# The inverse products of levels 1 to 4 as 32 by 32 tiles instead of 64 by 64 quarters, in a gated delta-rule layer

## What is computed

```python
St = St * jnp.exp(gt)[..., None]
err = jnp.einsum('bhk,bhkv->bhv', kt, St)
St = St + bt[..., None, None] * kt[..., None] * (vt - err)[..., None, :]
ot = jnp.einsum('bhk,bhkv->bhv', qt, St)
```

## Time and profile before

| | |
|---|---|
| median of 3 runs | 10145.46 us (10145.2 to 10145.66) |
| span of the profiled execution | 10143.4 us |
| TensorE matmul busy | 9551.0 us (94%) |
| VectorE busy | 7448.5 us (73%) |
| ScalarE busy | 6863.1 us (68%) |
| GpSimd busy | 3592.4 us (35%) |
| mean granted TensorE clock | 0.973 |

### The profile page before, as it was taken

How to read it: one execution, slowest core, us unless ns; L and a number is a source line. 1 busy time by engine, 2 the same in 40 slices (tenths; PEclk the granted TensorE clock), 3 DMA queues, 4 the chain that set the end, 5 groups by cost and what they waited for, 6 DMA issues and landing times. The chain is left out here.

```text
span 10143.4 us, 303836 instructions
## 1 busy us (share of the span) xinstructions
PE 9551.0 (94%) x104164; PEld 6538.4 (64%) x104164; DVE 7448.5 (73%) x13320; ACT 6863.1 (68%) x15797; POOL 3592.4 (35%) x5963
## 2 busy tenths in 40 slices
PE   4899999999999999999999999999999999996888
PEld 2566767677676766666767666676767666773333
DVE  2687878888788878787888878887888787882111
ACT  1677777777777777777777777777777777771111
POOL 0343434444344434443434434343444443440000
PEclk7899999999999999999999999999999999998999
DMA  1211111111111111111111111111111111111000
GB/s 29 50 38 35 37 35 36 36 35 38 35 37 36 36 36 36 36 37 35 37 35 37 36 34 38 35 37 35 36 36 35 36 36 35 38 35 33 8 8 12
DMA packets 513762, 347.45 MB, mean 34 GB/s; under 512 B 63136, under 2 KB 510752, under 8 KB 512816
## 3 DMA queue, kind: packets, MB, share of 16 engines
q1 hardware_dynamic: 511760, 328.31, 12.9%
q0 software_dynamic: 1088, 4.26, 0.1%
HBM read 289.94 MB, written 42.47 MB: 33 GB/s over the span
## 5 line engine op out<-in xcount | busy, mean ns | idle before, releaser
L1174 POOL TENSOR_TENSOR KB<-KB,tot 128x256 f32<-128x256 f32 x1290 | 1050.1, 814 | 4077.3 <-PE bank L601 4077.2
L1242 DVE SCALAR_TENSOR_TENSOR acc<-bank,hp,acc 128x510 f32<-128x510 f32 (+2 forms) x2331 | 1713.9, 744 | 76.5 <-ACT hnew L870 13.1
L554 PE MATMUL bank<-hn,w_qkv 128*128 (+1 forms) x3108 | 1527.7, 614 | 1.5 <-issue 1.5
L1349 DVE TENSOR_TENSOR invT<-invT,bank 64x128 f32<-64x128 f32 x2576 | 740.2, 287 | 541.3 <-PE bank L645 523.9
L1304 DVE COPY_PREDICATED BIG<-masks,bank 128x512 f32<-128x512 int32 x1032 | 1039.9, 1008 | 76.3 <-DVE BIG L1304 65.5
L887 ACT ACTIVATE Zm<-bank 64x128 f32<-64x128 f32 x2576 | 707.1, 274 | 519.2 <-PE bank L628 504.3
L628 PEld LDWEIGHTS bank<-invE,BIG 64*64 64x64 f32 x20624 | 702.6, 134 | 498.3 <-issue 436.1
L1316 DVE TENSOR_TENSOR QKF<-QKF,tot 128x512 f32<-128x512 f32 x1289 | 913.3, 709 | 16.3 <-PE bank L601 1.0
L645 PEld LDWEIGHTS bank<-invT,Zm 64*64 64x64 f32 x20608 | 707.7, 135 | 335.6 <-issue 287.0
L601 PE MATMUL bank<-QKF,KB 128*64 128x64 f32 x20640 | 886.9, 228 | 0.6 <-DVE QKF L1322 0.4
L653 PEld LDWEIGHTS bank<-ident,invT 128*128 128x128 f32 x5152 | 589.6, 141 | 431.6 <-DVE BIG L1304 271.7
(11 more groups left out here) (205 smaller groups left out, 20308.8 us busy)
## 6 DMA issues: line engine op xcount, KB each, us to landing
bb<-beta_rows SPq DMA_DIRECT2D x520, 128.0 KB, 4.1
states<-StC SPq DMA_DIRECT2D x288, 128.0 KB, 1.9
w_qkv<-in_L_attn_wk_dram SPq DMA_DIRECT2D x260, 128.0 KB, 2.3
w_qkv<-in_L_attn_wq_dram SPq DMA_DIRECT2D x260, 128.0 KB, 2.3
w_qkv<-in_L_attn_wv_dram SPq DMA_DIRECT2D x260, 128.0 KB, 2.2
StA<-states SPq DMA_DIRECT2D x259, 128.0 KB, 2.1
w_o<-in_L_attn_wo_dram SPq DMA_DIRECT2D x257, 128.0 KB, 2.1
w_fb<-in_L_attn_f_b_dram SPq DMA_DIRECT2D x260, 64.0 KB, 3.9
```

Source lines behind the costliest of these rows:

```text
L554: mm = eng.matmul(rows(BK["proj_" + "qkv"[n_]]), w_qkv[:, n_, k, :], hn_v[:, k, :, cols], start=(k == 0), stop=(k == KD - 1))
L1174: eng.tensor_tensor(e_, e_, t_.to_broadcast([P, C, P // (2 * m), m]), ALU.mult).then_inc(ev[f"kb_mul{s}"], 1)
L1242: eng.scalar_tensor_tensor(dst, rows(bk)[:, :, 0:BLK - sh], hp[par][:, w_:w_ + 1], dst, ALU.mult, ALU.add).then_inc(ev[("tap_" if t_ < 2 e ...
L1349: x_ = eng.tensor_tensor(o_, o_, ps[rw, :, h * QUART:(h + 1) * QUART].rearrange("p c (n m) -> p c n m", m=1 << s), ALU.subtract)
```

## The change

In levels 1 to 4 (`s < LEVELS - 2`, s from 1) the blocks are at most 32 rows, so the matrix is also block-diagonal in four tiles of 32 by 32. Each of z1 to z4 and y1 to y4 is now given as 16 matmuls: 4 chains by 4 tiles on the diagonal of the array, 32 rows of contraction, 32 columns of weights, 32 moving columns as before. Level 5 keeps the 64 by 64 quarters, level 6 its form. Nothing is moved: what stands before and behind each product on TensorE, and all other engines' instructions, stay as they were.

```diff
@@ z_product(s, tile)
                         if s == LEVELS - 1:
                             for ch in range(C):
                                 mm = eng.matmul(ps[HALF:, ch * HALF:(ch + 1) * HALF], Am[s][0:HALF, ch, HALF:], src[0:HALF, ch, :], start=True, stop=True)
+                        elif s < LEVELS - 2:
+                            for ch in range(C):
+                                for q4 in range(4):
+                                    rw, h = slice(q4 * QUART, (q4 + 1) * QUART), q4 // 2
+                                    mm = eng.matmul(ps[rw, ch * HALF + h * QUART:ch * HALF + (h + 1) * QUART], Am[s][rw, ch, rw],
+                                                    src[rw, ch, h * QUART:(h + 1) * QUART], start=True, stop=True)
                         else:
                             for ch in range(C):
                                 for h in range(2):
@@ y_product(s, tile, par)
                             for ch in range(C):
                                 mm = eng.matmul(ps[0:HALF, ch * HALF:(ch + 1) * HALF], Zm[s][HALF:, ch, 0:HALF], invT[par][HALF:, ch, HALF:],
                                                 start=True, stop=True)
+                        elif s < LEVELS - 2:
+                            for ch in range(C):
+                                for q4 in range(4):
+                                    rw, h = slice(q4 * QUART, (q4 + 1) * QUART), q4 // 2
+                                    half_of = slice(h * HALF, (h + 1) * HALF)
+                                    mm = eng.matmul(ps[rw, ch * HALF + h * QUART:ch * HALF + (h + 1) * QUART], Zm[s][rw, ch, rw],
+                                                    invT[par][rw, ch, half_of].rearrange("p (n two m) -> p n two m", two=2, m=1 << s)[:, :, 1, :],
+                                                    start=True, stop=True)
                         else:
                             for ch in range(C):
                                 for h in range(2):
```

## The result

The kernel with the change takes **9956.78 us** by median (9947.83 to 9965.62, 4 runs) against 10145.56 before (10145.2 to 10146.03): ratio 0.9815, 95% interval 0.9801 to 0.9829, 189 us less. The prediction was 9900, and its range held the time. The profiled execution is the fastest of the four, 9947.83 us with a span of 9946.0; before, the runs lay within 0.8 us of each other, now within 18.

The account below looks back on a forecast made before the run. TensorE, busy 33.14 of a 33.66 us step, was taken as the bound. 258 tiles x (0.90 + 0.05) us = 245 us off 10145 gave 9900 us; forecast's own range 9785 to 9980, full range 9780 to 10290.

Parts of the forecast that it names:

- The pace is the load of the columns; four corners run at once: Each changed product: loading 32 columns takes 0.030 us a pass, four corners together, so its TensorE slot is 0.40 us, 0.18 less.
- Half way: Rival: corners overlap but passes start only every 12 ns, slot 0.50 us, 115 us saved, 10030 us; chance 0.14.
- fixed cost: Rival: a pass costs 0.058 us whatever it loads, slot 0.60 us, 10200 to 10220 us; chance 0.10 shared with two corners running together.
- two at a time: Rival: only two corners run together, slot 0.62 us, 10200 to 10220 us; chance 0.10 shared with a fixed pass cost.
- one file: Rival: TensorE is handed passes only every 0.029 us, so 32 need 1.05 us a product, 11130 us; chance 0.13.
- y1 with y6, 0.13 more: These two products lose their overlap on TensorE because tile sizes differ: 1.00 us together instead of 0.87.
- z1 and y1 give nothing, the wait before state 0 takes it: Their sum of -0.05 us only lengthens TensorE's 0.23 us wait before state 0, so nothing reaches the step's end.
- 102.0 us before L683 (state) in 264 times [...] about 0.4 [...] a step: TensorE's wait before the state matmuls in the long phase, read as about 0.4 us in every step.
- z3, up to 0.10 and counted 0.05: Between solve 1 and outputs: a shorter z3 lets outputs start at most 0.10 us earlier, counted as 0.05 a step.
- 5 x 0.18 = 0.90 a step: z2, y2, y3, z4 and y4 each save 0.18 us that reaches the step's end, 0.90 us a step.
- All of their cost lies in the slots above. Nothing else is added on any engine or queue.: Issue: the 64 more matmuls per tile on TensorE cost nothing beyond the products' slot times.
- a sign of a cause left out: In the profile after, a granted clock below 1.00 in the step would show a cause the forecast omitted.

Follow-up runs that it names:

- rows64: The whole change, but each small matmul takes the 64 rows of its quarter (added rows zeros), still 32 columns of weights: 9964.1 us.
- corner_major: The whole change with the two loops swapped, all four chains of one corner before the next corner: 10652.53 us.
- five: The whole change with only z2, z4, y2, y3 and y4 in 32 by 32 tiles; z1, z3 and y1 back in quarters: 9905.93 us.
- three: The kernel before with only z1, z3 and y1 put into 32 by 32 tiles: 10158.57 us.
- seven: The whole change without y1, which goes back to quarters; z1 to z4 and y2 to y4 stay 32 by 32: 10073.34 us.

## Why the prediction came out as it did

The change is faster, as forecast, and the range held the time; the forecast lay 57 us too low.

- **The pace is the load of the columns; four corners run at once**: right. 0.032 us a pass where 0.030 was estimated, slot 0.38 where 0.40 stood. rows64 shows that it is the columns; the load as their reason is still argued. Half way, fixed cost, two at a time and one file are all refuted. corner_major adds a case that the list lacked: with the loops the other way round the same tiles lose 5%.
- **y1 with y6, 0.13 more**: right, 0.99 against 1.00, and five brings 0.87 back. The reason, unequal tile sizes, is borne out by two pairs (32 by 32 and 64 by 32 ahead of 64 by 64).
- **z1 and y1 give nothing, the wait before state 0 takes it**: right: 0.32 for 0.23 us, and three and five have the steps of before and of the change.
- **"102.0 us before L683 (state) in 264 times [...] about 0.4 [...] a step"**: misread. A step's wait is 0.23 us; 42 us of that row are eight waits at turns of the loop, and its longest wait, 5.7 us, is one of them. The waiting for instructions that the forecast left out stood in this row.
- **z3, up to 0.10 and counted 0.05**: too much. The 0.10 us between the copy's end and outputs is still there in the profile after; it is the hand-over and not a late TensorE.
- **5 x 0.18 = 0.90 a step**: the 0.90 came out by luck, of two errors that cancel: slots shorter than estimated, and losses behind them that the sum put at nothing. In the median of the steps without a turn or stall the slots went from 0.585 to 0.383 us, so they gave 5 x 0.20 = 1.01. The wait before turn5 took 0.04 of it (0.32 for 0.28 us), and level 5 with the diagonal, right behind y3, takes 1.17 us where it took 1.08; outputs' first group is 0.02 shorter.
- **"All of their cost lies in the slots above. Nothing else is added on any engine or queue."** This step failed. 64 more matmuls a tile are 4.2 MB more instructions on a queue that I hadn't read, and with them turns and stalls took 37 us more in the profiled execution, part of it TensorE waiting for instructions and part the granted clock of 0.50 behind the turns and many of the stalls, which the prediction named only as a sign of a cause left out. The median run lies 11 us above that execution's span where it lay 2 above before, 9 more. With the step's 0.90 for 0.95 (some 14 us), and less the 3 us gained ahead of the phase, that is the distance of 57 to the forecast. five, which adds less, came to 239 us where the sum said 245.

## What to carry to other kernels

Count what a product's tile loads, not what it computes: with few moving columns, halving the columns of the weights and handing the corners out side by side took a product from 0.59 to 0.38 us. Then convert only the products that reach the end of a step: the three that didn't were worth nothing, and the kernel without them is 51 us faster. When instructions are added to a streamed loop, read the page's instruction queue, the "issue" waits inside single groups and the granted clock behind them, and measure a longer body too.

## What I had not expected of the hardware

- The same 16 matmuls take 0.38 us with the corners interleaved and 0.82 one corner after the other.
- A body with fewer instructions can be slower: seven took 10073 us, with 56 dead matmuls in front of each body 9925, and with eight live ones more a tile 9957.
- The 15 turns of a long loop cost 139 us before the change, 1.4% of the kernel, and only 59 us of that are idle time: the granted clock is 0.50 for 7 to 14 us behind each turn. Part is also the blocks' own matmuls at seven of the turns.
- All 56 stalls in the middle of seven's bodies end 1.2 to 1.6 us after a packet of instructions has landed.
